# A two-layer tower in fp32: the first attention as one sequence of 128 units, with the projections of the next batch laid between them

## The reference, cut to what matters

```python
h = event_table[event_idx] + value_table[value_idx] + (tanh(x * w1 + b1) @ w2 + b2) * mask
z = layernorm(h)
Q, K, V = split_heads(z @ Wq + bq), split_heads(z @ Wk + bk), split_heads(z @ Wv + bv)
mu, var = mean(Q), mean((Q - mu) ** 2)                 # over the 16 of a head
nf = abs(Q - mu).sum() / (sqrt(var + EPS) + EPS)
omega = (|Q|^2 + |K|^2 - 2 QK) / (exp(-nf) + 1)
A = softmax(QK / sqrt(16) - omega)                     # 512 x 512 per head
h = h + merge_heads(A @ V) @ Wo + bo
```

## Time and profile before

| | us |
|---|---|
| median of 3 runs | 1368.13 |
| lowest and highest | 1366.05, 1370.78 |
| the profiled execution | 1377.66 |
| its span, first to last instruction | 1375.9 |

### The profile page before, as it was taken

How to read it: one execution, slowest core, us unless ns; L and a number is a source line. 1 busy time by engine, 2 the same in 40 slices (tenths; PEclk the granted TensorE clock), 3 DMA queues, 4 the chain that set the end, 5 groups by cost and what they waited for, 6 DMA issues and landing times.

```text
span 1375.9 us, 24081 instructions
## 1 busy us (share of the span) xinstructions
PE 1090.5 (79%) x7848; PEld 835.0 (61%) x7848; DVE 1043.6 (76%) x3087; ACT 688.7 (50%) x1457; POOL 483.3 (35%) x402
## 2 busy tenths in 40 slices
PE   2288585785964798788898878789899898969998
PEld 2255454554643778776787778556565565656675
DVE  3577695776928999999999999288586776845587
ACT  1366584665813344333343433177485675825433
POOL 7354372543710243224322434245162442620000
PEclk9789698997987889999999999899999999988999
DMA  3210000000000000000000001200000000000000
GB/s 79 69 72 1 0 0 0 0 0 0 1 31 1 1 2 2 1 2 1 2 1 2 2 1 40 77 1 1 0 0 0 0 0 0 1 1 1 1 8 23
DMA packets 6425, 14.63 MB, mean 11 GB/s; under 512 B 1855, under 2 KB 4482, under 8 KB 5762
## 3 DMA queue, kind: packets, MB, share of 16 engines
q1 hardware_dynamic: 5314, 11.42, 2.4%
q0 software_dynamic: 1024, 2.10, 0.6%
HBM read 12.47 MB, written 1.05 MB: 10 GB/s over the span
## 4 chain that ended last, share of the span: by engine, by line
DVE 34%; issue 31%; PE 24%; POOL 5%; DVEq 3%; ACT 3%; DMA 0%; POOLq 0%; SPq 0%; ACTq 0%
DVE one_u L897 5%; DVE w_v L891 5%; PE quad L1070 4%; DVE a_eT L694 4%; DVE i L829 3%; PE quad L1322 3%; PE bank L1317 3%; PE quad L1082 3%; POOL wu L345 2%; DVE vals L906 2%; DVE m L822 2%; DVE bi L845 2%; POOL a_en L363 1%; DVE one_v L888 1%; DVE a_negmax L681 1%
## 5 line engine op out<-in xcount | busy, mean ns | idle before, releaser
L363 POOL TENSOR_TENSOR a_en<-a_e,a_rrec 128x512 f32<-128x512 f32 x256 | 265.2, 1040 | 302.6 <-DVE a_rrec L688 292.5
L395 POOL TENSOR_TENSOR vals<-relu_in,g_sb 128x512 f32<-128x512 f32 x80 | 145.3, 1844 | 316.3 <-ACT g_sb L554 290.6
L681 DVE TENSOR_REDUCE a_negmax<-bank 128x1 f32<-128x512 f32 x256 | 175.9, 690 | 41.7 <-PE bank L1268 25.3
L427 ACT ACTIVATE a_e<-bank,a_negmax 128x512 f32<-128x512 f32 x256 | 176.0, 688 | 61.9 <-DVE a_negmax L681 51.1
L1070 PE MATMUL quad<-ident,a_en 128*128 128x128 f32 x1024 | 163.9, 284 | 44.0 <-DVE a_eT L694 36.6
L1070 PEld LDWEIGHTS quad<-ident,a_en 128*128 128x128 f32 x1024 | 110.0, 143 | 136.7 <-issue 120.5
L694 DVE TENSOR_TENSOR a_eT<-quad,a_eT 128x512 fp32r<-128x512 f32 x256 | 172.3, 675 | 4.5 <-ACT a_eT L436 4.2
L1082 PE MATMUL quad<-a_eT,a_v 128*128 128x512 f32 x512 | 174.2, 431 | 1.0 <-DVE a_eT L694 0.9
L436 ACT CAST a_eT<-quad 128x512 fp32r<-128x512 f32 x256 | 147.8, 577 | 15.2 <-PE quad L1070 15.2
L1210 PE MATMUL bank<-xnT,wd 128*128 128x128 f32 x1024 | 129.1, 286 | 4.9 <-ACT relu_in L521 4.9
L1210 PEld LDWEIGHTS bank<-xnT,wd 128*128 128x128 f32 x1024 | 123.2, 197 | 8.7 <-ACT relu_in L521 7.8
(11 more groups left out here) (207 smaller groups left out, 1818.5 us busy)
## 6 DMA issues: line engine op xcount, KB each, us to landing
wd<-in_pk_down SPq DMA_DIRECT2D x1, 2048.0 KB, 8.2
wu<-in_pk_up SPq DMA_DIRECT2D x1, 2048.0 KB, 13.2
wu<-in_moe_w SPq DMA_DIRECT2D x2, 1024.0 KB
out<-h SPq DMA_DIRECT2D x4, 256.0 KB, 2.3
wd<-in_num_rows SPq DMA_DIRECT2D x1, 512.0 KB
vals<-in_pk_wqT SPq DMA_DIRECT2D x1, 512.0 KB
vals<-in_pk_keys SPq DMA_DIRECT2D x1, 512.0 KB
wd<-in_a_wq SPq DMA_DIRECT2D x1, 512.0 KB
```

The source lines that it names most:

```text
L363: nc.gpsimd.tensor_tensor(m.en[:, s % 3, :], m.e[:, s % 3, :], m.rrec[:, s % 4:s % 4 + 1].to_broadcast([P, S]), ALU.mult).then_inc(a.nr, 1)
L395: nc.gpsimd.tensor_tensor(*weigh_args(t, c, k, g_sb[:, slot, :])).then_inc(vals_pool, 1)
L427: nc.scalar.activation(m.e[:, s % 3, :], bank[LOGITS[s % 3]][:, :], ACT.Exp, bias=m.negmax[:, s % 4:s % 4 + 1], accum_out=m.rowsum[:, s % ...
L681: V.tensor_reduce(m.negmax[:, s % 4:s % 4 + 1], bank[LOGITS[s % 3]][:, :], AX.X, ALU.max, negate=True).then_inc(a.mx, 1)
```

## The change

The first attention no longer uses `attention`, `AttentionMemory` and `Fori`. Each engine runs one written-out sequence of 128 units (`NU0`), numbered on through the batches, so the pipeline of one batch runs into the next. `heads0` is cut into steps, each tied to a unit number L (0 to 32) of the batch before: `heads0_pe`, `heads0_dve`, `heads0_act` and `heads0_pool` are called after the unit's own instructions. The first batch is prepared by the same steps ahead of unit 0. The output projection stands at L = 12 of the next batch, its addition at L = 13.

The preparation itself changes too. The joint weights get a fourth block of 128 columns, the query weights less their mean per head, so the product (512 columns now) gives the centred queries at once. Queries and keys are no longer split before their transposes: `q_aug` and `k_aug` hold every head twice (POOL makes the second copy, 18 of 32 columns), two heads are transposed together, and what comes out is split on its way from PSUM: keys into a hi part (ACT) and a lo part (DVE), queries into hi rows and lo rows of one tile (ACT, then DVE with a mask of rows). So there are 8 groups of four transposes instead of 16, and a unit has two products of 64 rows instead of one of 128. In batches after the first, all of this passes through PSUM bank 7 (twice bank 4). The values stand in two alternating tiles, whose 10240 elements per partition DVE clears at the start, ahead of the first embedding. Embedding is done batch by batch; the gathers of batch 1 stand in the preparation of batch 0, those of batches 2 and 3 between the units of batches 0 and 1, from L = 16 on. SP loads the joint weights and biases earlier, and the two big tables after the embedding of batch 3.

```diff
+    NU0 = B * UNITS
+    PAIRS, SLOTS = H // 2, 6
+    VB = HPG * (P + AUG)
...
-        wqkv0 = sb("wqkv0", [P, 3 * D])
-        bqkv0 = sb("bqkv0", [P, 3 * D])
+        qkv_wb = sb("qkv_wb", [P, 2, 4 * D])
+        q_mean = sb("q_mean", [P, 2, H])
...
-        mB = AttentionMemory("a0", sB, 1)
+        qT0 = sB.sb("a0_qT", [P, SLOTS, S], F32R)
+        kT0 = sB.sb("a0_kT", [P, SLOTS, 2, S], F32R)
+        v0 = sB.sb("a0_v", [P, 2, TPB * H // HPG, VB], F32R)
...
+        def qkv_bank(n, j):
+            return 7 if n else j
+
+        def chunk_bank(n, u):
+            return (7, 7, 7, 7, 7, 4, 7, 4)[u] if n else (4, 5, 6, 7, 0, 1, 2, 3)[u]
...
+            sp.dma_start(wqkv0[:, 0:3 * D], a0_wqkv).then_inc(ld_qkv, 16)
+            sp.dma_start(bqkv0[:, 0:3 * D], a0_bqkv.partition_broadcast(P)).then_inc(ld_qkv, 16)
...
+            def heads0_pool(n, L):
+                if L == 4:
+                    rstd_step(lnB, n, TPB)
+                if L == 17:
+                    pool.wait_ge(k_sum, n + 1)
+                    pool.wait_ge(ka_copied, n + 1)
+                    nc.gpsimd.tensor_copy(k_aug[:, :, :, 1, 0:DH0 + 2], k_aug[:, :, :, 0, 0:DH0 + 2]).then_inc(k_dup, 1)
+                if 18 <= L < 18 + TPB:
+                    j = L - 18
+                    if j == 0:
+                        pool.wait_ge(sig2, n + 1)
+                    nc.gpsimd.tensor_tensor(st0[:, 2, j], st0[:, 1, j], phalf[:, 0:H], ALU.pow).then_inc(sigma, 1)
+                if n == 0 and 20 <= L < 24:
+                    gather_event(TPB + L - 20)
+                if L == 25:
+                    pool.wait_ge(q_rdy, n + 1)
+                    nc.gpsimd.tensor_copy(q_aug[:, :, :, 1, 0:DH0 + 2], q_aug[:, :, :, 0, 0:DH0 + 2]).then_inc(q_dup, 1)
+                if n == 0 and 26 <= L < 30:
+                    gather_value(TPB + L - 26)
+
...
+            for L in range(32):
+                heads0_pool(0, L)
+            for s in range(NU0):
+                normalise0(s)
+                b, L = s // UNITS, s % UNITS
+                if b + 1 < B:
+                    heads0_pool(b + 1, L)
+                if b + 2 < B and L >= 16:
+                    t = (b + 2) * TPB + (L - 16) // 4
+                    if L % 4 == 0:
+                        gather_event(t)
+                    if L % 4 == 2:
+                        gather_value(t)
             pool.wait_ge(a0.add, B)
...
+                for u, at in enumerate((20, 22, 24, 26, 28, 29, 30, 31)):
+                    if L == at:
+                        c = n * PAIRS + u % PAIRS
+                        act.wait_ge(augT_ps, n * 2 * PAIRS + u + 1)
+                        if c >= SLOTS:
+                            act.wait_ge(a0.qk, 8 * (c - SLOTS + 1))
+                        dst = kT0[:, c % SLOTS, 0, :] if u < PAIRS else qT0[:, c % SLOTS, :]
+                        nc.scalar.copy(dst, bank[chunk_bank(n, u)][:, :]).then_inc(augT_hi, 1)
...
+            for s in range(NU0 + 9):
+                if s < NU0:
+                    exp0(s)
+                if 0 <= s - 3 < NU0:
+                    expT_hi0(s - 3)
+                if s - 8 > 0 and (s - 8) % (TPB * HPG) == 0:
+                    outT0((s - 8) // (TPB * HPG) - 1)
+                b, L = s // UNITS, s % UNITS
+                if b + 1 < B:
+                    heads0_act(b + 1, L)
...
+            dve.wait_ge(ld_qkv, 32)
...
+            V.memset(v0[:].bitcast(F32), 0.0).then_inc(v_zero0, 1)
...
+                    if L == 10 + 2 * j:
+                        dve.wait_ge(qkv_ps, n * TPB + j + 1)
+                        if n and j == 0:
+                            dve.wait_ge(v0_hi, n)
+                        V.tensor_tensor(qkv0[:, j, :], bank[qkv_bank(n, j)][:, :], bqkv0, ALU.add).then_inc(qkv_sb, 1)
...
+                for u, at in enumerate((21, 23, 25, 27, 29, 30, 31, 32)):
+                    if L == at:
+                        c = n * PAIRS + u % PAIRS
+                        dve.wait_ge(augT_hi, n * 2 * PAIRS + u + 1)
+                        src = bank[chunk_bank(n, u)][:, :]
+                        if u < PAIRS:
+                            V.tensor_tensor(kT0[:, c % SLOTS, 1, :], src, kT0[:, c % SLOTS, 0, :].bitcast(F32),
+                                            ALU.subtract).then_inc(augT_lo, 1)
+                        else:
+                            part = qT0[:, c % SLOTS, :]
+                            V.scalar_tensor_tensor(part, part.bitcast(F32), half_mask[:, 0:1], src,
+                                                   ALU.mult, ALU.add).then_inc(augT_lo, 1)
+
...
+            for s in range(NU0 + 4):
+                if s < NU0:
+                    rowmax0(s)
+                if 0 <= s - 1 < NU0:
+                    invert0(s - 1)
+                if 0 <= s - 4 < NU0:
+                    expT_lo0(s - 4)
+                b, L = s // UNITS, s % UNITS
+                if L == 0 and 0 < b < B:
+                    heads0_dve(b, 32)
+                if b + 1 < B:
+                    heads0_dve(b + 1, L)
+                if L == 13 and b:
+                    residual0(b - 1)
+            residual0(B - 1)
...
+                hd, j = s % UNITS // TPB, s % TPB
+                c, rows = s // UNITS * PAIRS + hd // 2, slice(hd % 2 * (P // 2), (hd % 2 + 1) * (P // 2))
+                if s % (2 * TPB) == 0:
+                    pe.wait_ge(augT_lo, s // UNITS * 2 * PAIRS + PAIRS + hd // 2 + 1)
+                if s >= 3:
+                    pe.wait_ge(a0.ex, s - 2)
+                for part in range(2):
+                    last = mm(bank[LOGITS[s % 3]][:, :], qT0[rows, c % SLOTS, j * P:(j + 1) * P], kT0[rows, c % SLOTS, part, :],
+                              start=(part == 0), stop=(part == 1))
+                last.then_inc(a0.qk, 1)
...
+                        mm(bank[qkv_bank(n, j)][:, :], xnT[:, j * P:(j + 1) * P], wqkv0, start=True, stop=True).then_inc(qkv_ps, 1)
+                for u, at in enumerate((21, 23, 25, 27, 29, 30, 31, 32)):
+                    if L == at:
+                        if u == 0:
+                            pe.wait_ge(k_dup, n + 1)
+                            pe.wait_ge(qkv_sb, (n + 1) * TPB)
+                        if u == PAIRS:
+                            pe.wait_ge(q_dup, n + 1)
+                        if n and u:
+                            pe.wait_ge(augT_lo, n * 2 * PAIRS + (u if u <= PAIRS else u - 1))
+                        if n and chunk_bank(n, u) == 4:
+                            pe.wait_ge(a0.ots, 2 * (n - 1) + 1)
+                        src = k_aug if u < PAIRS else q_aug
+                        for j in range(TPB):
+                            last = tp(bank[chunk_bank(n, u)][:, j * P:(j + 1) * P],
+                                      src[:, j, u % PAIRS * 2:u % PAIRS * 2 + 2].rearrange("p h r a -> p (h r a)"), ident[:])
+                        last.then_inc(augT_ps, 1)
...
+            for s in range(NU0 + 8):
+                if s < NU0:
+                    logits0(s)
+                if 0 <= s - 3 < NU0:
+                    expT0(s - 3)
+                if s >= 8:
+                    pv0(s - 8)
+                b, L = s // UNITS, s % UNITS
+                if L == 0 and 0 < b < B:
+                    heads0_pe(b, 32)
+                if b + 1 < B:
+                    heads0_pe(b + 1, L)
+                if L == 12 and b:
+                    project0(b - 1)
             project0(B - 1)```

On PE, a unit before is one product for the logits (`a_kT`, `a_qT`: keys and queries), four transposes of the normalised exponents (`a_en`) and two products with the values (`a_v`). The product with the joint weights (`wqkv`) stands behind all units of the batch, and the output projection (`wo`) behind it:

```order
L1070 MATMUL quad<-ident,a_en 128x128 [waits a0_expT_lo,a0_exp_normalised]
L1070 MATMUL quad<-ident,a_en 128x128 x3
L1082 MATMUL quad<-a_eT,a_v 128x512 x2
L1090 REGISTER_ALU
L1124 MATMUL bank<-a_kT,a_qT 128x512 [waits a0_exp_done]
...
L1134 MATMUL bank<-wqkv,xnT 128x384 [waits lnB_xnT_in_sbuf]
L1134 MATMUL bank<-wqkv,xnT 128x384
L1134 MATMUL quad<-wqkv,xnT 128x384 x2
```

428 lines of the change are left out of this document (237 added, 191 removed).

## The result

The changed kernel takes 1382.44 us (median of 7 runs), where the kernel before takes 1368.21 on the same chip: a ratio of 1.0097, 95% interval 1.0075 to 1.0119. It is **slower by 1%**, not faster by 3.2%. The ratios are of executions in the chip's faster state; one of the seven here (1432.42) was in the slower one. The profiled execution took 1380.1 us with a span of 1378.3. On a second chip the ratio was 1.0128 (1.0102 to 1.0153).

The account below looks back on a forecast made before the run. DVE bounds the units, an engine-to-engine chain the preparations. Start 58, batches 72, 76.6 and 75.6, last batch 51 and tail 13.6 sum to 346.8 for 391.1 us, 44.3 less; taken from the median 1324, range 1298 to 1352.

Parts of the forecast that it names:

- Ahead of the first unit: Preparation of batch 0: first unit at 58 us, 20 less than now, without the wait behind 16 gathers.
- the first term: The start up to the first unit, 58 us for 78.2 now.
- A unit: First attention's unit with two logits products of 64 rows: 1.46 us without steps laid in, range 1.38 to 1.46.
- A preparation laid between units: Steps laid between units: DVE stays the bound, 19.5 us on top of 43.8, meetings 7.6, so 71 per batch.
- the 7.6 for the meetings: Waits of engines for each other where preparation steps are laid between units: together 7.6 us per batch.
- rival 2: Gathers on POOL hold up PE's results: mild, 24 cost 30 us, 1354 (0.10); severe, 101 us, 1425 (0.06).
- the late results: Ahead of the first unit, PE's results came 3.5 to 4.2 us apart while POOL issued gathers.
- rival 3: DVE operations reading two SBUF tiles and POOL's multiplication exclude each other: 25 us at most, half 12, 1336; chance 0.08.
- rival 1: Waits between engines in steps laid between units add up: 14 more per batch, 1367; half of that, 1345; chance 0.14.
- rival 4: Meetings in steps between units are free, DVE catching up in the next: 3 x 7.6 us less, 1301; chance 0.12.
- What is hidden: The two 2 MB tables loaded after batch 3's embedding are free; loading twice the code at the start stays covered.

## Why the prediction was wrong

The stage was to end at 346.8 and ends at 391.7, 44.9 later. It divides as follows.

- **Ahead of the first unit: right for the changed kernel, wrong for the one before.** 59.7 for 58 (1.7). DVE starts its clear of the values at 16.13, after a gap of 2.08 that I had not counted. (The product with the joint weights, which I read as one at the low clock, ran at a granted 1.00 in the kernel before.) But "20 less than now" compared with 78.21, a start that the median does not have. The regular one is 66.7, and the regular stage ends at 379.5. I had named this danger in one clause ("part of the first term is not in the median") and had then subtracted all 44.3 from the median. With the regular start it would have been 32.7, so 1335.
- **A unit: the step that failed.** "I take 1.46 where nothing is laid in", between 1.38 and 1.46. The nearest row had two products of 128 rows, and I treated 64 rows as the same thing. Measured: 1.71 at the upper clock, of which 0.28 are the two changes of rows: with two products of 128 rows the same unit takes 1.55, and TensorE waits in it. The bounds were too low as well: 1.46 and 1.38 are means over 31 steps, of which the first have no `pv`; in the middle of a batch the kernels have 1.55 and 1.43. "No row has a product of 64 rows" should have widened the range upward, which my range did not.
- **The clock: no term at all.** The forecast has the fall from 0.97 to 0.72 between batches and no rival in which the units run at the lower level. They ran there for a third of the stage, at 3.05 us for a unit without a step (as at 256.0) and 3.9 and more with one, for 1.71 at the upper level. Both together, measured by two products of 128 rows against the changed kernel: 3.4, 11.3, 14.3 and 4.7 us in the four batches, **33.6 of the 44.9**. The last batch is at the upper level in both, so 4.7 is the price of the longer unit; four times that is 19, which leaves some 15 us to the clock. That split is an estimate: no run changes the one without the other. The sum is steadier than its parts: in the second profile of the changed kernel the loss is 8.5, 13.5, 9.4 and 4.6, 36.0 in all.
- **A preparation laid between units: close in sum.** With 128 rows the batches are 74.4, 81.1, 76.7 and 52.6, for 72, 76.6, 75.6 and 51, 9.6 us more. The two sources below come to more than that, so some other part of my 71 us per batch was too long, perhaps the 7.6 for the meetings. No run measures the meetings by themselves.
- **Gathers, rival 2.** Its basis fell with the late results. Between units they cost some 2 and 3 to 5 us in batches 0 and 1, not 1 each: that much is gone with earlier places, or with none between units. Mild, and far from its 30 us.
- **POOL and DVE exclude each other, rival 3: it happens, though I gave it 0.08.** POOL's multiplication and DVE, from the changed kernel:

```profile
117.29 1.81 DVE L881 TENSOR_TENSOR st<-st 128x32 f32<-128x32 f32 x1
...
292.04 1.72 DVE L872 TENSOR_TENSOR a_v<-qkv,a_v 128x128 fp32r<-128x128 f32 x4
```
```profile
116.92 1.04 POOL L365 DMA_INDIRECT wu<-in_value_table,idx_v  x1 [0.17 <-issue]
117.99 1.05 POOL L418 TENSOR_TENSOR a_en<-a_e,a_rrec 128x512 f32<-128x512 f32 x1
...
291.97 1.04 POOL L418 TENSOR_TENSOR a_en<-a_e,a_rrec 128x512 f32<-128x512 f32 x1
```

  Four steps of 0.28, 0.9 together, take 1.72 at 292.04: the first of them starts just behind the multiplication and takes 1.11. A step of 0.19 takes 1.81 and ends with the multiplication, at 119.1, but it starts while POOL still issues a gather, and in batch 2, without gathers, it took 0.19. So part of what gathers cost between units is this. Summed over the steps that were stretched (L752, L825, L872, L877, L881, L884) it is 13 us, 4.7 and 5.0 in the batches with gathers and 3.1 in the one without; I had 12. What it adds to the program's time is not shown, since TensorE and not DVE is the bound there. The earlier trace rows show a stacking that POOL's power did not hold up, and I let that row speak for all of POOL. The Trainium skill, SBUF — State Buffer, section SBUF: two separate sides, has the exclusion for a GpSimd operation that reads SBUF. The trace agrees for the multiplication (1.11 for 0.28) and not for the power; the lesson is to look for the row with the right partner.
- **Meetings cost more, rival 1:** not needed. **Meetings are free, rival 4:** no.
- **What is hidden.** The tables cost nothing that shows. On the loading of code no run was made.

The sign was wrong because the two large terms, 33.6 for the rows and 11.6 for the unusual start, are as large as the whole gain forecast; the 9.6 and the 1.7 us on top make it the 12 us by which the stage is longer than the regular one (391.7 for 379.5).

## What to carry to other kernels

A product on fewer rows is another kind of product, not a cheaper one (here one of 64 rows between products of 128 made the unit 1.53 us, one of 128 rows 1.43): count how often the rows change in the order of TensorE, put products of one kind together where there are several, and look at the granted clock of the stretch, since a TensorE without a gap may be one at its lower level. When a cost has no row, bound it upward too, by what the engine would do at its lower clock. And before a gap in a profiled execution becomes a term, ask whether the median of the other runs has room for it: here the profile was 9.5 us above it, and the late start was 11.5.
